# Two heads' value products accumulated in one column group of a decoder layer kernel

## What is computed

```python
def _L0_attn_ref(x, Wq, Wk, Wv, Wff, bff):
    q = x @ Wq.T * (1.0 / jnp.sqrt(jnp.asarray(D, x.dtype)))
    k = x @ Wk.T
    v = x @ Wv.T
    ...
    scores = jnp.einsum('bqhd,bkhd->bhqk', q, k)
    attn = jax.nn.softmax(scores, axis=-1)
    out = jnp.einsum('bhqk,bkhd->bqhd', attn, v).reshape(B, S, D)
    return out @ Wff.T + bff
...
x = x + _L0_attn_ref(_layernorm(x, axis=-1), ...)
x = x + _L0_xattn_ref(_layernorm(x, axis=-1), ctx_1024, ctx_1024, mask_BxSxS2_if1, ...)
x = x + _L0_ffn_ref(_layernorm(x, axis=-1), ...)
```

## Time and profile before

| | us |
|---|---|
| median of 3 runs | 1232.64 (1230.56 to 1234.49) |
| the profiled execution | 1227.32 |
| its span, first to last instruction | 1225.6 |
| PE busy | 1032.1 (84%) |
| DVE busy | 872.8 (71%) |
| ACT busy | 844.0 (69%) |
| POOL busy | 553.9 (45%) |
| mean granted PE clock | 0.931 of full |

### The profile page before, as it was taken

How to read it: one execution, slowest core, us unless ns; L and a number is a source line. 1 busy time by engine, 2 the same in 40 slices (tenths; PEclk the granted TensorE clock), 3 DMA queues, 4 the chain that set the end, 5 groups by cost and what they waited for, 6 DMA issues and landing times. The chain is left out here.

```text
span 1225.6 us, 32468 instructions
## 1 busy us (share of the span) xinstructions
PE 1032.1 (84%) x11795; PEld 796.9 (65%) x11795; DVE 872.8 (71%) x2569; ACT 844.0 (69%) x1729; POOL 553.9 (45%) x550
## 2 busy tenths in 40 slices
PE   2467799999999999999999999967518999999940
PEld 1255667777777777777777777745416888887730
DVE  2655657778788787797887785654366888888846
ACT  1155468778777777777787777734417999998940
POOL 4312223245545544544554544433432666665650
PEclk9877889999999999999999999988758999999985
DMA  4327564473474454554544642230454222322219
GB/s 97 90 81 161 133 157 98 116 181 93 121 173 105 124 153 121 127 142 117 142 122 118 152 105 58 73 78 28 149 170 152 79 76 82 84 78 77 80 49 365
DMA packets 119326, 144.24 MB, mean 118 GB/s; under 512 B 33944, under 2 KB 98360, under 8 KB 114240
## 3 DMA queue, kind: packets, MB, share of 16 engines
q1 hardware_dynamic: 107824, 120.37, 38.2%
q0 software_dynamic: 9168, 17.21, 4.5%
q10 hardware_dynamic: 2176, 4.59, 1.0%
HBM read 88.42 MB, written 55.36 MB: 117 GB/s over the span
## 5 line engine op out<-in xcount | busy, mean ns | idle before, releaser
L583 ACT ACTIVATE probs<-sc_a 77x512 f32<-77x512 f32 (+1 forms) x512 | 301.0, 591 | 122.7 <-PE sc_a L997 51.9
L1291 POOL DMA_INDIRECT y_d<-yo,row x156 | 160.2, 1027 | 123.0 <-issue 68.2
L730 DVE TENSOR_REDUCE negm_m<-sc_m 128x4 f32<-128x512 f32 x256 | 174.0, 684 | 43.8 <-PE sc_m L981 42.1
L730 DVE TENSOR_REDUCE negm_cm<-sc_m 128x4 f32<-128x308 f32 x256 | 119.8, 474 | 107.2 <-PE sc_m L986 102.0
L456 POOL DMA_INDIRECT xs_d<-xrow,slot_i x128 | 128.1, 1001 | 140.1 <-PE sc_a L1002 109.0
L1017 PE MATMUL pv<-probs,big 128*32 128x128 f32 x4096 | 165.6, 281 | 0.3
L1386 DVE TENSOR_TENSOR gl<-g,gh 128x512 fp32r<-128x512 f32 x156 | 107.5, 690 | 38.2 <-ACT g L1335 30.2
L1017 PEld LDWEIGHTS pv<-probs,big 128*32 128x32 f32 x4096 | 97.3, 110 | 54.7 <-issue 36.6
L981 PE MATMUL sc_m<-ks,qs 96*128 96x128 bf16 x1024 | 104.6, 229 | 31.5 <-DMA ks<-stk_k 13.8
L981 PEld LDWEIGHTS sc_m<-ks,qs 96*128 96x128 bf16 x1024 | 72.9, 101 | 77.5 <-issue 50.0
L997 PE MATMUL sc_a<-cqs,cks 102*77 102x128 bf16 x1024 | 101.4, 222 | 6.4 <-DMA cqs<-cmscr 5.9
(11 more groups left out here) (201 smaller groups left out, 2511.5 us busy)
## 6 DMA issues: line engine op xcount, KB each, us to landing
xg<-xs_d SPq DMA_DIRECT2D x39, 260.0 KB
stk_q<-parts_q SPq DMA_DIRECT2D x16, 384.0 KB, 2.5
stk_k<-parts_k SPq DMA_DIRECT2D x16, 384.0 KB
qs<-stk_q SPq DMA_DIRECT2D x16, 384.0 KB
ks<-stk_k SPq DMA_DIRECT2D x32, 192.0 KB
stk_cq<-parts_cq SPq DMA_DIRECT2D x16, 384.0 KB, 2.9
cqs<-stk_cq SPq DMA_DIRECT2D x16, 384.0 KB, 5.4
xin<-x_dram SPq DMA_DIRECT2D x16, 256.0 KB
```

What stands on the lines that cost most here:

```text
L583: nc.scalar.activation(probs[e % 4][0:rows], sc_a[e % 2][0:rows], ACT.Exp, scale=scale)\
L730: nc.vector.tensor_reduce(out=negm[n][:, s, g, 4 * half:4 * half + 4], in_=sc_m[u % 2][:, 0:4 * cols].rearrange("p (j k) -> p j k", j=4), ...
L1291: nc.gpsimd.indirect_dma_start(out=y12_d, in_=yo[par][:, c, :], in_offset=None, bounds_check=2 * B * S - 1, oob_is_err=False, out_offset=b ...
```

## The change

The two heads of a pair (one of each group g) share one column group. The first writes its 8 values and its ones column in columns 0 to 15 of 32 and zeros in 16 to 31, the second has them in 16 to 31 and zeros in 0 to 15, and it is added onto the first in PSUM (`start=(g == 0), stop=(g == 1)`). A bank so holds two sequences. Output copies, sets of transposes and divisions are two per phase in place of four: `out_T` after unit 11 and at the end, `outputs_T` and `divide` at steps 0 and 1. A division has 32 reciprocals a lane and 32 x 8 products. The number and shape of the value products stay. The value weights' columns and `bv` are reordered on the host, and `bv_b` is loaded for four sequences.

```diff
+OW = VW // NG
+NO = NS // 2
...
-        bv_b = sb("bv_b", [SC, D])
+        bv_b = sb("bv_b", [SC, NS, D])
...
-        vaug, cvaug = ([big[:, g + i].rearrange("p (s h w) -> p s h w", s=NS, h=H) for i in range(2)] for g in (0, 2))
+        vaug, cvaug = ([big[:, k + i].rearrange("p (q g w) -> p q g w", g=NG, w=VW) for i in range(2)] for k in (0, 2))
...
-        oT = dict.fromkeys("sc", sa("oT", [128, NS, T]))
+        oT = dict.fromkeys("sc", sa("oT", [128, NO, T]))
...
-                  (bv_b, xbv.unsqueeze(0).broadcast_to([SC, D])),
+                  (bv_b, xbv.unsqueeze(0).unsqueeze(0).broadcast_to([SC, NS, D])),
...
+        def in_pair(tile):
+
+            return tile.rearrange("p q g w -> p q (g w)").rearrange("p q (a b) -> p q a b", b=OW)[:, :, 0:4:3, :]
...
-                            if e % 4 == 3 and e > 4:
-                                out_T(n, b, e // 4 - 1)
+                            if e == 11:
+                                out_T(n, b, 0)
                         between(u)
                     if on_(b):
-                        out_T(n, b, NS - 1)
-
-                def out_T(n, b, s):
-                    act.wait_ge(pv_ok[n].sem, pv_ok[n].val(b, 4 * s + 4))
-                    nc.scalar.activation(oT[n][:, s, :], pv[s % 2][:], ACT.Copy).then_inc(oT_ok[n].sem, 1)
+                        out_T(n, b, 1)
+
+                def out_T(n, b, k):
+                    act.wait_ge(pv_ok[n].sem, pv_ok[n].val(b, 8 * k + 8))
+                    nc.scalar.activation(oT[n][:, k, :], pv[k][:], ACT.Copy).then_inc(oT_ok[n].sem, 1)
...
-                            nc.scalar.activation(vaug[par][:, :, :, 0:DH], wb[0][:].rearrange("p (s h i) -> p s h i", s=NS, h=H),
+                            nc.scalar.activation(in_pair(vaug[par])[:, :, :, 0:DH],
+                                                 wb[0][:].rearrange("p (q g i) -> p q g i", g=NG, i=DH),
                                                  ACT.Copy).then_inc(drained["v"].sem, 1)
...
+                def divide(n, b, k):
+
+                    key, half = f"oTT_{n}", slice(2 * k, 2 * k + 2)
+                    dve.wait_ge(filled[key].sem, filled[key].val(b, k + 1))
+                    v = wb[k][:].rearrange("p (h w) -> p h w", w=OW)
+                    r = rden[n][:, half].rearrange("p s h -> p (s h)")
+                    nc.vector.reciprocal(r, v[:, :, DH]).then_inc(rden_ok[n].sem, 1)
+                    dve.wait_ge(rden_ok[n].sem, rden_ok[n].val(b, k + 1))
+                    nc.vector.tensor_tensor(out=on[n][:, half].rearrange("p s h i -> p (s h) i"), in0=v[:, :, 0:DH],
+                                            in1=r.unsqueeze(2).broadcast_to([128, 2 * H, DH]),
+                                            op=ALU.mult).then_inc(drained[key].sem, 1)
...
-                        if u < NS and on_(t - 3):
+                        if u < NO and on_(t - 3):
                             divide("c", t - 3, u)
...
-                    if u % 4 == 0 and s >= 2:
-                        pe.wait_ge(oT_ok[n].sem, oT_ok[n].val(b, s - 1))
-                    elif u % 4 == 0:
-                        wait_block(pe, oT_ok[last[0]], last[1], s + 3)
+                    if u % 8 == 0:
+                        wait_block(pe, oT_ok[last[0]], last[1], u // 8 + 1)
+                    slot = 2 * (s % 2) + half
                     for c in range(4):
-                        i = nc.tensor.matmul(pv[s % 2][32 * c:32 * c + VW, (u % 4) * S:(u % 4 + 1) * S],
-                                             va[:, s, HG * g + 4 * half + c, :],
-                                             probs[u % 4][:, c * S:(c + 1) * S], start=True, stop=True)
+                        i = nc.tensor.matmul(pv[s // 2][VW * c:VW * (c + 1), slot * S:(slot + 1) * S],
+                                             va[:, HG * s + 4 * half + c, g, :],
+                                             probs[u % 4][:, c * S:(c + 1) * S], start=(g == 0), stop=(g == 1))
...
+                def outputs_T(n, b, k):
+
+                    key = f"oTT_{n}"
+                    claim(k, key, b, k + 1)
+                    pe.wait_ge(oT_ok[n].sem, oT_ok[n].val(b, k + 1))
                     for slot in range(4):
-                        i = nc.tensor.transpose(wb[s % 2][:, slot * S:(slot + 1) * S],
-                                                oT[n][:, s, slot * S:(slot + 1) * S], ident[:])
-                    i.then_inc(filled[k].sem, 1)
+                        i = nc.tensor.transpose(wb[k][:, slot * S:(slot + 1) * S],
+                                                oT[n][:, k, slot * S:(slot + 1) * S], ident[:])
+                    i.then_inc(filled[key].sem, 1)
```

More of the change, by code:

```diff
@@ L232, in program @@
         pv_ok = {n: sem(f"pv_{n}_ok", UNITS) for n in ("s", "c")}
-        oT_ok = {n: sem(f"oT_{n}_ok", NS) for n in ("s", "c")}
-        rden_ok = {n: sem(f"rden_{n}_ok", NS) for n in ("s", "c")}
+        oT_ok = {n: sem(f"oT_{n}_ok", NO) for n in ("s", "c")}
+        rden_ok = {n: sem(f"rden_{n}_ok", NO) for n in ("s", "c")}
         ss_ok = sem("ss_ok", 2)
@@ L733, in maxima @@
                         between(u)
[L735 to L742, removed]
-                                            in1=rden[n][:, s, :].unsqueeze(2).broadcast_to([128, H, DH]),
-                                            op=ALU.mult).then_inc(drained[k].sem, 1)
+                def divide(n, b, k):
[8 more added lines that the diff above has]
+                                            op=ALU.mult).then_inc(drained[key].sem, 1)
                 def add_residual(n, b, res, dst):
@@ L838, in in_x @@
                             nc.vector.tensor_tensor(
-                                out=cvaug[1 - par][0:SC, :, :, 0:DH],
-                                in0=wb[0][0:SC, :].rearrange("p (s h i) -> p s h i", s=NS, h=H),
-                                in1=bv_b[:].rearrange("p (h i) -> p h i", h=H).unsqueeze(1).broadcast_to([SC, NS, H, DH]),
+                                out=in_pair(cvaug[1 - par])[0:SC, :, :, 0:DH],
+                                in0=wb[0][0:SC, :].rearrange("p (q g i) -> p q g i", g=NG, i=DH),
+                                in1=bv_b[:].rearrange("p s d -> p (s d)").rearrange("p (q g i) -> p q g i", g=NG, i=DH),
                                 op=ALU.add).then_inc(drained["cv"].sem, 1)
@@ L869, in in_y @@
                     def in_y(u):
-                        if u < NS and on_(t):
+                        if u < NO and on_(t):
                             divide("s", t, u)
@@ L1535 @@
     by_place = np.array([h * DH + i for i in range(DH) for h in range(H)])
-    by_slot = np.array([(HG * g + 4 * u + c) * DH + i for u in range(2) for g in range(2) for c in range(4)
+    by_slot = np.array([(HG * g + 4 * u + c) * DH + i for u in range(2) for c in range(4) for g in range(2)
                         for i in range(DH)])
```

14 lines of the change are left out of this document (5 added, 9 removed).

## The result

The changed kernel takes 1235.8 us (median of 20 runs, 1228.1 to 1242.3), the kernel before 1231.8 (20 runs, 1229.1 to 1235.9): a ratio of 1.0034 with a 95% interval of 1.0018 to 1.0050. It is 4 us slower; the forecast was 3.4 us faster. The profiled execution after is the fastest of its twenty: 1228.1 us, span 1226.3, mean granted clock 0.920 (before: 1227.3, 1225.6, 0.931). So the two profiles alone, read by their spans, would say that nothing happened.

A forecast was written before the change was run, and what follows sets the result against it. DVE's maxima of unit 2 were taken to hold PE at self phase starts, cross phases nearer PE's pace. Terms -5.5 + 2.1 + 2.6 + 1.0 + 0.9 + 1.2 + 1.8 - 0.7 gave 3.4 us gained: 1229.2, range 1219 to 1243.

The forecast's parts named there:

- rival (b): Self phases' starts: PE has less work, so the clock falls, nine times 1.7 us; 11.9 us slower, 1244.5; chance 0.21.
- Self phases: Starts of 12 self phases: larger divisions delay unit 2's maxima and unit 4's scores by 0.46 us each; 5.5 us lost.
- PE sets the pace again from unit 5 on: Self phases after unit 4: DVE is ahead again and PE sets the pace as before.
- I take 0 here: ACT's vanished output copies at units 7 and 15: hidden by PE's work, 0 gained, at most 2 us.
- Cross phases: Unit 4's scores earlier: five phases gain 0.11 us each, five 0.31; three at PE's pace gain 2.6 us together.
- Ends: Serial chains outside the paired phases: fewer divisions gain 0.9 us in body 0, 1.2 in body 16, 1.8 in 17 and 18.
- Constants: Start: larger `bv_b` load ahead of `temp_b` in SP's queue, for which ACT waits; 0.7 us lost (0 to 1.1).
- Accumulation: Value products: the second head's adding onto the first's costs 0.
- the moved wait: PE's wait for the last output copy, at step 1 instead of 3: 0; uncovered up to 0.6 us in 30 phases.
- the strides: Writes of `vaug` with other strides and the same 512 elements: 0, bounds 0.1 either way for 32 writes.
- Rival (a): PE bounds the phase starts too, so all removed transposes come off: 28 us, 1204.6; chance 0.05.
- (c): ACT's relief from fewer copies counts and divisions are cheap: about 10 us gained, 1222.5; chance 0.17.

The follow-up runs named there:

- short: Kernel before with two of ACT's four output copies per attention cut from 512 to 16 columns from batch element 1 on; ratio 1.0002.
- late: Kernel before plus an idle DVE operation of about 0.23 us ahead of the divisions at steps 0 and 1 of each self phase; ratio 1.0064.
- busy: Changed kernel plus four idle PE transposes at each of steps 2 and 3 of every self phase; ratio 0.9962.
- busys: Changed kernel with idle PE transposes at self phase steps 2 and 3 and the small bias load spread by a DVE copy; ratio 0.9913.
- thin: Kernel before with three of four output transposes left out at steps 2 and 3 of each self phase; ratio 1.0003.
- thin0: Kernel before with one 8-row transpose in place of each set of four at steps 2 and 3 of the self phases; ratio 1.0033.
- both: Kernel before with idle DVE work ahead of step 0 and 1 divisions and three of four transposes left out at self phase steps 2 and 3; ratio 1.0067.
- at13s: Changed kernel with divisions and output transposes at steps 1 and 3 and the small bias load; ratio 0.9860, second measurement (at13s_2) 0.9883.
- at13: Changed kernel with divisions and output transposes at steps 1 and 3 of each phase, large bias load; ratio 0.9914, second measurement (at13_2) 0.9905.
- self13s: Changed kernel with small bias load and divisions and output transposes at steps 1 and 3 in self phases only; ratio 0.9877.
- both0: Kernel before with idle DVE work ahead of step 0 and 1 divisions and one 8-row transpose per set at self phase steps 2 and 3; ratio 1.0103.
- at03: Changed kernel with the second pair's output transposes and division at step 3 of each phase instead of step 1; ratio 1.0024.
- small: Changed kernel with the bias loaded as in the kernel before and spread over four sequences by one DVE copy; ratio 1.0038.
- anew: Changed kernel with every value product started anew, nothing accumulated, and value tile padding 1.0 in place of 0.0; ratio 1.0076.
- again: The changed kernel itself, unaltered, measured once more against the kernel before; ratio 1.0031.

## Why the prediction was wrong

**The step that failed is the choice between the forecast and rival (b).** The sum has no term for the clock, and the forecast expected it at 1.00 from 200 to 750 us; it fell six times there, which cost 9.3 us. The mechanism of (b) is right in place, sign and kind: the clock falls at the self phases' starts, where PE has been given less to do. Its size was near: 9 falls of 1.7 us forecast, 6 of 1.4 to 1.8 seen in the first profile and 5, one of them double, in the second. Its chance, 0.21, was too low. The argument against it was that the trace of before shows no fall there. But that trace had 0.45 us idle at this place, and the change makes it 1.92. The prediction counted PE's pieces of work ("five where it has seven") and did not add up the idle time between them, though every term for it stood in the sum: 0.88 us of transposes removed and 0.46 us of delay added. The kernels of this study in order of that idle time:

| kernel | PE idle at most self phases' starts, us | falls, 200 to 760 us, in the profile | clock loss, median us, this / before |
|---|---|---|---|
| before | 0.45 | 0 | |
| short | 0.45 | 0 | 83.1 / 83.1 |
| late | 0.61 | 0 | 82.5 / 81.8 |
| busy | 0.88 | 0 | 83.0 / 80.7 |
| busys | 0.91 | 0 | 81.6 / 83.6 |
| thin | 0.98 | 0 | 83.2 / 81.8 |
| thin0 | 1.14 | 3 | 86.4 / 83.2 |
| both | 1.22 | 2 | 80.5 / 83.6 |
| at13s | 1.30 | 0 | 85.6 / 81.8 |
| at13 | 1.31 | 1 | 88.8 / 80.7 |
| self13s | 1.32 | 0 | 85.5 / 83.6 |
| both0 | 1.38 | 1 | 90.8 / 83.2 |
| at03 | 1.82 | 5 | 96.8 / 80.7 |
| small | 1.92 | 6, one double | 99.2 / 81.8 |
| anew | 1.92 | 6, one double | 103.9 / 80.7 |
| changed (again) | 1.98 | 5, one double | 101.3 / 83.6 |

at13_2 and at13s_2, with 1.30 us idle, have one fall each, neither at a self phase's start (263 and 719 us). The ends of the table are clear and its middle is not in order: at13s and self13s have more idle time than thin0 and no fall. Phases that look alike in the timeline fall in one body and not in the next, mostly in the same bodies from one profile to another; what picks them was not found. Of the changed kernel's 17.7 us more clock loss (101.3 - 83.6) about half is time: busy, which has 2.3 more, is 8.8 us faster than it. The Trainium skill ("TensorE: Matmul & The Clock Gate", "HAM oscillation") describes such falls for matmul groups parted by waits of 3 to 5 us for DMA. The kind of fall agrees with this trace, the length of the waits does not: here they are 0.45 to 0.8 us, for VectorE, three in a row, and the falls came all the same.

**Self phases, 5.5 us lost.** The division's growth (0.23 us), the delay (0.46) and unit 4's scores (3.45 us after the first maximum, 3.5 forecast) are as forecast, and late shows that such a delay can cost its full size. In the changed kernel it does not: without a fall the self phase lasts 22.25 us, before 22.26 in the mean of ten. Two sentences of the prediction failed: that PE sets the pace again from unit 5 on, and "I take 0 here" for ACT's copies. The delay is still whole at unit 9. Then, with the copy of unit 7 gone, a DVE instruction of 0.63 us shrinks to 0.17, and at unit 10 the delay is gone (13.54 us after the first maximum in both kernels). After that 0.32 us are lost behind POOL by unit 14 (18.26, before 17.94), and the rest of the phase takes 3.99 us where it took 4.48 in five and 4.0 in five. short shows the copies as the cause at unit 10; why the end is always the short one here was not tried. 5.5 us were forecast lost that were not.

**Cross phases, 4.7 us gained.** Maxima of unit 5 stand 5.62 us behind those of unit 0 after, 5.72 or 5.91 before: 0.10 and 0.29 gained, forecast 0.11 and 0.31. The whole phase is 24.70 us in the mean of ten, before 25.01 (the last of the ten is 1.2 shorter, the others some 0.2). The one at 216 us is 0.84 shorter, forecast 0.88. Right in its sizes.

**Ends.** Body 0's divisions take 92.03 to 93.69, 1.66 us, before 2.41: 0.75 gained, 0.9 forecast. From 720 us to phase B the two profiles close by 1.9 us; 3.0 were forecast. Roughly right.

**Constants, 0.7 us lost.** ACT starts 3.3 us later; what of it reaches the end is 3.7 us by the mean of four pairs and nothing by the changed kernel's own. The term was sized by issue time and by the pace of neighbours of 64 KB; the load repeats one row of 512 bytes 308 times where it was 77, and small puts the start back. The step that failed is that price: 3.3 us at ACT's start is 2.6 more, and above its own bound of 1.1.

**Accumulation, the moved wait, the strides: 0.** anew shows the first; PE waits 1.3 us in all for ACT's copies (the group of L1054), where up to 0.6 us in each of 30 phases had been the bound. Right.

Rival (a) fell with the maxima as releaser; of (c) the part on ACT is real but hidden. With the falls (9.3 us) in, the self phases' 5.5 out and the constants at 3.3, the sum is 3.4 + 5.5 - 9.3 - 2.6 = -3.0 us, against -4 measured. It is no proof: each of these is known to 1 or 2 us, and the constants' share less well. That the forecast missed by 7.4 us and not by 13 is luck: the 5.5 us that were not lost hide a part of what the clock cost.

## What to carry to other kernels

Before taking work off TensorE, add up the idle time that the edit leaves in the stretch, waits and removed work together, even where that work is hidden: here hidden transposes held the clock, and giving them back made the kernel 8.8 us faster. The sum warns and does not decide: at 1.1 to 1.4 us of idle time some kernels had falls and some none. A small operation on VectorE can wait for GpSimd's long one, so a delay or a gain ahead of it can vanish in that wait. Halving the number of small operations is not enough; place the larger ones so that they don't stand in one row ahead of the engine that paces. Here the same change is 0.34% slower with its divisions at steps 0 and 1, and 1.3% faster with them at steps 1 and 3 and a small load of the bias.

## What the runs showed of the hardware

An instruction of DVE on four elements took 0.17 us with POOL idle and up to 2.33 us where POOL was adding tiles in SBUF. The longest, in at13s, DVE and then POOL:

```profile
250.51 2.33 DVE L714 TENSOR_SCALAR lnve<-lnmv 128x4 f32<-128x4 f32 x1
252.75 0.68 DVE L740 TENSOR_REDUCE negm_m<-sc_m 128x4 f32<-128x512 f32 x1
```

```profile
250.44 1.15 POOL L448 TENSOR_TENSOR parts_m<-rest_k,parts_m 16x512 bf16<-16x512 f32 x1
251.56 1.25 POOL L443 TENSOR_TENSOR x2res<-x,bo_b 128x512 f32<-128x512 f32 x1
252.76 0.60 POOL L454 COPY xrow<-xrow 128x512 f32<-128x512 f32 x1
```

It sat through two of POOL's instructions and ended with the second, and the profile counts it as busy, not as waiting. The Trainium skill ("Trainium Architecture — The Big Picture", "What this means for kernel authors") says that VectorE and GpSimd contend for one pair of ports, by an exclusive lock. The rows above agree.

The time of a kernel with falls scatters more: 12 to 16 us between the lowest and the highest run for the changed kernel, anew and at03 (8 to 20 runs), 5 to 8 us for late, thin, busy and busys (6 to 12 runs); the kernel before has 5 to 11 us (17 to 25 runs). A single profile of such a kernel can miss the verdict by more than the change is worth.
